# A batched bilinear product in float32 on one core: the last 8 rows by matmuls over 128 partitions, two to a column tile in place of four

## The reference

```
bilinear = einsum('bie,ied->bid', feature, weight)   # x (512, 200, 64), w (200, 64, 64)
out      = einsum('bid,bjd->bij', bilinear, feature) # (512, 200, 200), float32
```

## Time and profile before

| what | value |
|---|---|
| median of 3 runs | 347.33 us (344.71 to 351.31) |
| the profiled execution's own time | 347.19 us |
| its span, first to last instruction | 345.4 us |
| mean granted TensorE clock | 0.930 |
| busy: TensorE matmuls, weight loads | 250.5 us (73%), 221.2 us (64%) |
| busy: VectorE, ScalarE | 148.4 us (43%), 128.3 us (37%) |
| DMA | 115.70 MB, mean 335 GB/s |

### The profile page before, as it was taken

The page is one execution under the profiler, slowest core; times in us unless marked ns, Lnnn a source line. Parts: engine busy times, 40 slices in busy tenths (PEclk is TensorE's granted clock), DMA queues, the critical chain, the costliest instruction groups (busy, mean ns, idle before and its releaser), DMA issues.

```text
span 345.4 us, 15674 instructions
## 1 busy us (share of the span) xinstructions
PE 250.5 (73%) x7296; PEld 221.2 (64%) x7296; DVE 148.4 (43%) x172; ACT 128.3 (37%) x177; POOL 2.4 (1%) x5
## 2 busy tenths in 40 slices
PE   0167679599967674969785967869985877987870
PEld 0156668378867573748775957748875766766760
DVE  0042455136634541605563553504653554635550
ACT  1032426045524422314452443403553444442540
POOL 2000000000000000000000000000000000000000
PEclk9987899899989988989998798989999999999995
DMA  7999998847999997757799999964899997746796
GB/s 302 423 426 423 400 368 280 331 193 289 351 409 399 395 388 261 236 242 291 300 374 418 395 366 421 306 286 194 335 373 390 407 386 312 289 199 260 284 408 286
DMA packets 21808, 115.70 MB, mean 335 GB/s; under 512 B 2416, under 2 KB 2416, under 8 KB 21360
## 3 DMA queue, kind: packets, MB, share of 16 engines
q1 hardware_dynamic: 21744, 114.70, 84.6%
HBM read 32.77 MB, written 81.92 MB: 332 GB/s over the span
## 4 chain that ended last, share of the span: by engine, by line
PE 72%; issue 19%; DMA 4%; DVE 1%; SPq 1%; ACT 1%
PE psum L238 46%; PE psum L210 16%; PE psum L255 9%; DMA w_sb<-w_dram 4%; PE psum L222 1%; DVE tile L270 1%; SPq L128 1%; ACT mixed L291 1%
## 5 line engine op out<-in xcount | busy, mean ns | idle before, releaser
L238 PE MATMUL psum<-x_sb,mixed 64*64 64x200 f32 x3072 | 173.2, 357 | 32.9 <-issue 29.5
L238 PEld LDWEIGHTS psum<-x_sb,mixed 64*64 64x64 f32 x3072 | 141.4, 143 | 49.5 <-issue 41.2
L270 DVE COPY tile<-psum 128x800 f32<-128x800 f32 x100 | 99.2, 992 | 141.2 <-PE psum L238 128.9
L270 ACT COPY tile<-psum 128x800 f32<-128x800 f32 x100 | 82.7, 827 | 117.2 <-PE psum L238 85.5
L210 PE MATMUL psum<-x_sb,w_sb 64*64 64x64 f32 x3072 | 67.7, 228 | 37.3 <-issue 21.3
L210 PEld LDWEIGHTS psum<-x_sb,w_sb 64*64 64x64 f32 x3072 | 65.6, 140 | 40.6 <-issue 39.5
L291 DVE COPY mixed<-psum 64x512 f32<-64x512 f32 x48 | 33.1, 689 | 28.2 <-PE psum L210 26.9
L291 ACT COPY mixed<-psum 64x512 f32<-64x512 f32 x48 | 27.9, 581 | 43.6 <-PE psum L210 43.0
L255 PE MATMUL psum<-x_sb,tails 64*32 64x200 f32 x1024 | 32.6, 377 | 13.0 <-issue 13.0
L255 PEld LDWEIGHTS psum<-x_sb,tails 64*32 64x32 f32 x1024 | 22.6, 115 | 21.7 <-issue 18.3
L293 ACT COPY mixed<-psum 128x512 f32<-128x512 f32 x24 | 14.1, 587 | 44.3 <-PE psum L210 44.2
## 6 DMA issues: line engine op xcount, KB each, us to landing
out_dram<-tile SPq DMA_DIRECT2D x96, 800.0 KB, 6.3
x_sb<-x_dram SPq DMA_DIRECT2D x16, 800.0 KB, 8.7
x_sb<-x_dram SPq DMA_DIRECT2D x32, 400.0 KB, 7.7
w_sb<-w_dram SPq DMA_DIRECT2D x2, 2048.0 KB, 16.7
out_tail_dram<-tile SPq DMA_DIRECT2D x4, 800.0 KB, 4.5
w_sb<-w_dram SPq DMA_DIRECT2D x1, 2304.0 KB, 22.5
```

The source lines that it names most:

```text
L238: last = nc.tensor.matmul(psum[half_rows(pair), n % BANK_PAIRS * 2 + h, a * FIELDS:(a + 1) * FIELDS], mixed[half_rows(h), (CHUNKS * g + c) ...
L270: copy(tile[:, k % SLOTS, engine], psum[:, bank:bank + 2, 0:2 * FIELDS]).then_inc(copied[engine], 1)
```

## The change

A tail matmul contracts over all 128 partitions. A weight window holds one sample of half 0 (its values in partitions 0 to 63, 8 columns) and one of half 1 (partitions 64 to 127, the next 8 columns), with zeros where the rows of one half meet the columns of the other. The four samples of a column tile are then two from each half, and take two accumulating matmuls in place of four. Per quad, `tails` holds 64 columns: the two samples of half 0 and half 1 at blocks 0 and 3 of four, zeros in between. A unit has 2 x 2 x 2 x 4 = 32 matmuls of 200 columns. The tail mix's result is copied by both engines, ScalarE the partitions of half 0, VectorE those of half 1. The tail output has the same size with its rows in another order, and the host reads it accordingly.

```diff
     def tail_mix(n, g):
-        add(n, 1, 0, "tail_mix", g)
+        add(n, 1, 1, "tail_mix", g)
...
-    tails = sb("tails", [128, HALF_SAMPLES // 4, 4, TAIL_TILE + TAIL])
+    tails = sb("tails", [128, QUADS, 2 * TAIL_TILE // (2 * TAIL), HALVES, TAIL])
...
-                for piece in range(2):
-                    for b in range(4):
-                        for tile4 in range(4):
-                            four = 8 * e + 4 * piece + tile4
-                            for h in range(HALVES):
-                                weights = tails[half_rows(h), four].rearrange("p b w -> p (b w)")
+                for half_unit in range(2):
+                    for piece in range(2):
+                        for pair in range(2):
+                            for column in range(4):
+                                quad = 16 * e + 8 * half_unit + 4 * piece + column
+                                weights = tails[:, quad].rearrange("p b h r -> p (b h r)")
                                 last = nc.tensor.matmul(
-                                    psum[tile4 * TAIL_TILE:(tile4 + 1) * TAIL_TILE, n % BANK_PAIRS * 2 + h,
-                                         piece * FIELDS:(piece + 1) * FIELDS],
-                                    weights[:, b * TAIL_TILE:(b + 1) * TAIL_TILE],
-                                    x_sample(g, h, 2 * four + b // 2, b % 2), start=b == 0, stop=b == 3)
+                                    psum[column * TAIL_TILE:(column + 1) * TAIL_TILE,
+                                         n % BANK_PAIRS * 2 + half_unit, piece * FIELDS:(piece + 1) * FIELDS],
+                                    weights[:, pair * TAIL_TILE:(pair + 1) * TAIL_TILE],
+                                    x_sb[:, g % 2:g % 2 + 2, quad, :, pair], start=pair == 0, stop=pair == 1)
...
             def tail_mix(n, g):
-                if engine == 0:
-                    eng.wait_ge(unit_ready, n + 1)
-                    eng.wait_ge(zeroed, 1)
-                    source = psum[:, n % BANK_PAIRS * 2, :].rearrange("p (r f b) -> p f b r", r=TAIL, b=4)
-                    copy(tails[:, :, :, 0:TAIL], source).then_inc(copied[engine], 1)
+                eng.wait_ge(unit_ready, n + 1)
+                eng.wait_ge(zeroed, 1)
+                source = psum[half_rows(engine), n % BANK_PAIRS * 2, :].rearrange(
+                    "p (r q b) -> p q b r", r=TAIL, q=QUADS)
+                copy(tails[half_rows(engine), :, 0:4:3, engine, :], source).then_inc(copied[engine], 1)
```

More of the change, by code:

```diff
@@ L335 @@
     rows = rows.transpose(0, 6, 2, 5, 7, 3, 1, 4, 8).reshape(GROUPS, HALVES, HALF_SAMPLES, TAIL_FIRST, FIELDS)
-    tail = r["out_tail_dram"].reshape(GROUPS, 4, 4, TAIL, 2, HALVES, 2, FIELDS)
-    tail = tail.transpose(0, 5, 4, 6, 1, 2, 3, 7).reshape(GROUPS, HALVES, HALF_SAMPLES, TAIL, FIELDS)
+    tail = r["out_tail_dram"].reshape(GROUPS, 4, 2, HALVES, TAIL, 2, 2, 2, FIELDS)
+    tail = tail.transpose(0, 3, 5, 6, 7, 1, 2, 4, 8).reshape(GROUPS, HALVES, HALF_SAMPLES, TAIL, FIELDS)
     whole = np.concatenate([rows, tail], axis=3)
```

## The result

| | median us | lowest to highest | runs |
|---|---|---|---|
| kernel before | 347.79 | 344.71 to 351.31 | 4 |
| changed kernel | 333.20 | 331.86 to 347.02 | 4 |

The ratio is 0.9604, 95% interval 0.9524 to 0.9684: the change saves 14.6 us by the medians, and 11.0 to 16.6 us by the interval.

A forecast was written before the change was run, and what follows sets the result against it. TensorE with its code fetches sets the pace around the tails. Idle time that can go, 14.2 us, less 1.6, plus 0.4 of array work gave 13.0: 347.2 to 334.2, 334.3 by the median; range 324 to 345.

The forecast's parts named there:

- What the gaps are: TensorE's issue gaps are waits for code pieces of 126 load-and-matmul pairs, one q8 packet each, fetched through shared DMA engines.
- The sign of being wrong: The whole reading would be wrong if TensorE's issue waits kept their sum with four code pieces fewer.
- The price of a 128x32 tail matmul: In tail units, four tiles run at once: 46 ns a pair, 2.9 us a unit against 3.0 before.
- Rival (c): 128-row tail tiles overlap only by two, 92 ns a pair, 5.9 us a unit: slower, 356 us; chance 0.08.
- Which idle time goes: Of chunk 1's 24.6 us idle time with drains, 10.4 stays, 14.2 can go; less 1.6, 12.6 us goes.
- the stall at the first tail unit of groups 0, 1 and 2: Chunk 1: these code stalls, 11.6 us with drains, stay except 1.2 us more cover in group 1, so 10.4 us.
- 1.6 for all other pieces: Chunk 1: a piece with a whole mix unit falls 0.4 us short of its fetch, one per group, 1.6 us.
- The clock: Chunk 1 loses 6.4 us to lowered clock; stalls over 3 us stay, so 0 saved, perhaps 2.7 in group 1.
- Rival (b): Given back: chunk 2's fetches take longer or piece phase shifts; half the gain lost, 341 us, up to 346.5; chance 0.22.
- Rival (a): Every removed code piece takes its interval along, 17.9 to 24.2 us gain, say 326 us; chance 0.12.
- The rule that crossing a block of code is mostly hidden: Skill's rule on TensorE's code fetches: only the array's 0.8 us would go; the prediction said the trace disagrees.

The follow-up runs named there:

- first job of the experiments: Changed kernel unchanged, rerun for a second profile beside the kernel before: 333.6 us, 12.7 under the kernel before, ratio 0.963.
- pad_tail: Changed kernel with one needless single-column matmul behind each tail matmul, 512 pairs put back: 348.1 us, ratio to the kernel before 1.012.
- half_work: Kernel before with two of the four tail matmuls of each column tile left out, tail output incomplete: 331.5 us, ratio 0.969.
- execution of 347.0: First profiled execution of the changed kernel, nothing altered, a disturbed one: 347.0 us.
- 330.1 us execution: Second profiled execution of the changed kernel, nothing altered: 330.1 us, 3.5 under its median of 333.6.
- one_copy: Changed kernel with both copies of the tail mix on ScalarE, none on VectorE: 336.8 us, ratio to the kernel before 0.964.
- after_shift: Changed kernel with its first mix unit computed twice, so later code pieces end half a piece earlier in the work: 334.4 us.
- its shifted form: Kernel before with its first mix unit computed twice, 64 pairs more at the start: 351.8 us, 1.0125 times as long.
- pad_chunk2: Changed kernel with 512 needless single-column pairs behind the score matmuls of chunk 2: 345.7 us, 12.1 over the changed kernel.

## Why the prediction was right

The forecast was 334.3 us, a gain of 13.0; measured were 333.2 and 14.6 (and 12.7 in the first job of the experiments). The cause was right. That the number came so close is partly luck, as two of its terms were wrong and stood against each other.

*What the gaps are.* Right, and shown: pad_tail put back the instructions without the work and the gain was gone, of which about 10 us as idle time for code and the clock that went with it; half_work took away 11.5 us of work at equal code and gained 2 at most. The sign of being wrong, issue waits that keep their sum, did not come: 63.8 us fell to 55.1, and to 59.9 in the execution of 347.0. In the four stretches of chunk 1 they fell from 18.4 to 6.7.

*The price of a 128x32 tail matmul.* Right: 47 ns a pair against the 46 taken, four tiles beside each other. Rival (c) is out; its 92 ns did not occur.

*Which idle time goes.* The sum was right, the step under it was not. 12.6 us of chunk 1's idle time with the drains at its gaps were to go. By the same count the four stretches have 10.1 us of idle time in 8 gaps, 10.1 + 8 x 0.3 = 12.5 of 24.6, so 12.1 went. But the prediction says "What of it stays: the stall at the first tail unit of groups 0, 1 and 2", 10.4 us, and counts only 1.6 for all other pieces. In the 330.1 us execution none of the three stalls stands, and the 12.5 us are in eight other gaps, two of which (3.2 us) are waits for copies of the mix. In the 347.0 us execution two of the three stand, with up to 5.1 us. Which stalls stay was wrong, and that their sum was right is luck.

*The clock.* Counted at 0, with up to 2.7 us more if a stall shrank. In the 330.1 us execution the stretches have 1.00, 0.94, 1.00 and 1.00, a loss of 0.06 x 28.1 = 1.7 us to the level of 1.2 GHz where it was 6.4, so 4.7 us came back: 12.1 of idle time and drains and 4.7 of clock make up 16.8 of the 18.2 us of chunk 1. The term was put at 0 because the stalls over 3 us were to stay. That the clock falls only with such stalls is not borne out either: the stretch at 0.94 has no wait over 2.1 us. Counted over the three profiles named below, the loss is 1.7, 3.4 and 1.9 us against 6.4 and 5.0, so 3.4 us came back on the mean.

*Given back.* Rival (b) is in it with a small share, as far as single executions can show it. Chunk 1 gained 18.2 us in this execution, more than the kernel. Over the profiles of the changed kernel, of one_copy and of after_shift, chunk 1 sums to 102.5, 104.5 and 102.4, against 120.7 and 118.8 of the kernel before and its shifted form: 16.6 us less. The sum of chunk 1 in one_copy, and of chunk 0 in after_shift, as windows:

```profile
...
sum 104.50, PE 93.16; mean PE 23.29
```

```profile
...
sum 111.50, PE 77.01; mean PE 19.25
```

Chunk 0 took 110.2, 109.3 and 111.5 against 108.0 and 109.7, so 1.5 us more; chunk 2 took 77.6, 81.4 and 82.5 against 79.0 and 80.5, 0.8 more. 16.6 - 1.5 - 0.8 = 14.3 us, near the 14.6 of the medians. The first profile of the changed kernel (112.9, 115.8 and 79.8 us in chunks 1, 0 and 2) is not in these means, and 1.5 and 0.8 are well within what single executions differ by. So two errors of the prediction, the clock left out (3.4 us on the mean) and nothing taken off for chunks 0 and 2 (2.3), stood against each other.

*Rival (a)*, every piece at its interval: out as a forecast of the time. It asked for a gain of 17.9 to 24.2 us, and the interval of the result ends at 16.6. For heavy traffic, where it would matter most, pad_chunk2 leaves it open.

*The rule that crossing a block of code is mostly hidden* (the Trainium skill, Runtime: NRT & Kernel Launch, Instruction fetch mechanics) would have given 0.8 us. The runs contradict it for this kernel, where the same DMA engines are 0.6 to 1.0 busy with data: 10 us for four blocks in pad_tail, with what the clock has in it. The issue waits fall from 63.8 to 29.6 us when the stores are quartered.

## What to carry to other kernels

When TensorE shows idle time that no semaphore ends, count instructions between the gaps: at a constant count, with one packet of the code queue to each, they are fetches of code, as here, and then matmuls are to be paid by the piece as well as by the column, so that filling a tile shape with fewer, taller matmuls gains where the array's work stays the same. Such a gain is sized by the idle time of the stage where the instructions go, not by the number of pieces times the mean interval, and the granted clock has a share of its own (3.4 us here). Expect some us of play: the same program took 330.1 and 347.0 us in two executions, with stage sums up to 10 us apart, so a stage needs more than one profile before its sum is trusted.

## What was not expected of the hardware

A stall for code of 3 to 5 us in the same unit of the same program is there in one execution and missing in another. Two executions of one program differed by 17 us, of which 14 are TensorE's busy time at a granted clock of 0.899 against 0.947. Quarter stores left 29.6 us of issue waits, 6.5 of them in chunk 1 at a DMA share of 0.36 to 0.43, so a fetch isn't free even then. And with 1.6 MB of loads a group moved from one stage into an emptier one, a third stage was 7 to 12 us longer in the one execution profiled, for a reason that stays open.
